# Last dense rounds of ACT and PE as engine loops, gathered rows in four paced groups, router constants loaded first

## The chip, the core and the metric

One core of a Trainium2 chip runs the whole program. The metric is the device time of one execution in microseconds. The engines are PE (TensorE), DVE (VectorE), ACT (ScalarE), POOL (GpSimd) and SP (SyncE, here a queue for transfers); they run on their own and order themselves by semaphores alone: an instruction raises a semaphore when it ends (`then_inc`), another engine waits for a value (`wait_ge`).

## What is computed

A decoder layer over x (4 batches, 512 tokens, 256 wide): a state space block, cross attention to a context, and a mixture of experts, each added to its input and normalized. The change touches the last part alone:

```python
def _ffn(x, w1, w2, w3):
    return jax.nn.silu(x @ w1.T) * (x @ w3.T) @ w2.T
shared = 0
for i in range(2):                          # two experts for all tokens
    shared = shared + _ffn(xf, sw1[i], sw2[i], sw3[i])
logits = xf @ router_w.T + expert_bias
rw, sel = jax.lax.top_k(logits, 2)          # two of eight experts for each token
rw = jax.nn.softmax(rw, axis=-1)
out = sum(combine[:, e] * _ffn(xf, w1[e], w2[e], w3[e]) for e in range(8)) + shared
x = _layernorm(x + out)
```

## The kernel before

`experts` (from L1286) works in three stages, each engine with its program in one block.

The first shared expert runs in dense rounds n = 0 to 3, one for each batch b of 512 tokens. A round has MT = 4 blocks of 128 hidden columns. PE's `hidden(n, m)` (L1805) multiplies the turned tokens by w1 and w3 into one of two PSUM buffers; each product is made of three terms of high and low parts (`xth`, `xtl`, `wh`, `wl`), so a block has 12 matmuls of 512 columns. ACT takes the silu (`activate`, L1523), DVE multiplies (`gate_on`, L1651), ACT copies the high part (`gate_high`, L1531), DVE forms the low part (`gate_low`, L1657), and PE's `down(n, m)` (L1826) multiplies by w2: 12 matmuls of 256 columns. PE's order in a round is hidden 0, 1, 2, down 0, hidden 3, down 1, 2, 3. Hidden block u waits for the gate of block u - 2. After a round DVE adds the four tiles of the result to the rows (`add_dense`, L1665), each as soon as `o_done` says so.

Beside these rounds DVE ranks the router's logits and lists the tokens of each expert. The second stage runs the chosen experts over SLOTS = 39 tiles of 128 gathered tokens: POOL gathers the rows (L1486, at most 3 tiles ahead), PE turns and multiplies them with weights addressed through a register, and SP stores each result tile to `y_dram` (L1443).

The third stage is the second shared expert: rounds n = 4 to 7, in the same form. When all result tiles are stored, POOL gathers the rows back (L1496): for each batch b, 4 tiles of tokens times 2 choices, 8 gathers of 128 rows of 1 KB, which all raise `y_fetched[b]`. The 32 gathers follow one another with no wait between. Behind them on POOL stand the four `pow` of the last normalization (L1501), one for each batch. DVE adds the gathered rows, weighted, in `add_chosen(b)` (L1683), which waits for `y_fetched[b]`, and normalizes in `normalize(b)` (L1700), which waits for POOL's `pow`. DVE's order puts these between the gates: batch 0 is added after round 5, batch 1 at (6, 2) with `normalize(0)` behind it, batch 2 at (7, 1) with `normalize(1)`, batch 3 at (7, 3) with `normalize(2)`; batch 3 is normalized last. SP stores each batch (L1446).

Ahead of the first stage SP issues, in this order, three weight loads of 512 KB (L1425), the router's weights and the bias (L1426, L1427), four stores of the rows (L1429), and the loads of all experts' weights into `wall` (L1435, "the wall loads"). PE's first transpose (L1895) waits for router and bias (`consts_loaded`); ACT splits the first weight (L1507) and then copies the turned tokens (`xth`, L1513).

Of the kernel before, what the change touches and what calls it, by code (L numbers as in the profile page):

```python
# [19 lines left out]
ACT = mybir.ActivationFunctionType  # L20
AX_X = mybir.AxisListType.X

P = 128
B, S, DM = 4, 512, 256
TT = S // P
KD = DM // P
# [1250 lines left out]
E, NSH, TOPK, HID = 8, 2, 2, 512  # L1277
MT = HID // P
NTILE = B * TT
SLOTS = B * S * TOPK // P + E - 1  # L1280
# [5 lines left out]
def experts(nc, router_t, expert_bias, w1_t, w3_t, w2_t, x2, out):  # L1286
    x2_dram = nc.dram_tensor("e_x2_dram", (NTILE * P, DM), F32, kind="Internal").ap()
    y_dram = nc.dram_tensor("e_y_dram", (SLOTS * P, DM), F32, kind="Internal").ap()
    with ExitStack() as ctx:
# [6 lines left out]
        ps_h = ctx.enter_context(nc.psum_tensor("e_h", [P, 2, 2, 512], F32))  # L1296
        ps_o = ctx.enter_context(nc.psum_tensor("e_o", [P, TT, 512], F32))

        wall = sb("e_wall", [P, E, 3, 1024])
        xth = sb("e_xth", [P, KD, B * S], F32R)  # L1300
# [112 lines left out]
        def use(n, m):  # L1413

            return n * MT + m + (SLOTS if n >= B else 0)
# [3 lines left out]
        @block.sync  # L1419
        def _(sp):  # L1420
            by_rows = lambda w, e: w[e].rearrange("(k p) n -> p k n", p=P)
            cols = (HID, HID, DM)
            tables = (w1_t, w3_t, w2_t)
            for j in range(3):
                sp.dma_start(raw_first[j].rearrange("p (k n) -> p k n", n=cols[j]), by_rows(tables[j], E)).then_inc(first_loaded[j], 16)  # L1425
            sp.dma_start(router[:], router_t.rearrange("(k p) e -> p k e", p=P)).then_inc(consts_loaded, 16)  # L1426
            sp.dma_start(bias[:], expert_bias.partition_broadcast(P)).then_inc(consts_loaded, 16)  # L1427
            for b in range(B):
                sp.dma_start(x2_dram[b * S:(b + 1) * S].rearrange("(t p) d -> p t d", p=P),  # L1429
                             x2[:, b * TT:(b + 1) * TT]).then_inc(x2_stored, 16)  # L1430
            for e in range(E):
                if e == 6:
                    sp.wait_ge(ids_done, 1)
                for j in range(3):
                    sp.dma_start(wall[:, e, j].rearrange("p (k n) -> p k n", n=cols[j]),  # L1435
                                 by_rows(tables[j], e)).then_inc(wall_loaded, 16)
            for j in range(SLOTS):
                if j in (0, 10, 18):
                    i = (0, 10, 18).index(j)
                    sp.wait_ge(w_split, 3 + i)  # L1440
                    sp.dma_start(raw[:].rearrange("p (k n) -> p k n", n=cols[i]), by_rows(tables[i], E + 1)).then_inc(raw_loaded, 16)
                sp.wait_ge(y_read, j + 1)
                sp.dma_start(y_dram[j * P:(j + 1) * P], y_row[:, j % 2]).then_inc(y_stored[j % 2], 16)  # L1443
            for b in range(B):
                sp.wait_ge(x3_ready, b + 1)
                sp.dma_start(out[b].rearrange("(t p) d -> p t d", p=P), x3[:, b * TT:(b + 1) * TT]).then_inc(stored, 16)  # L1446
            sp.wait_ge(stored, 16 * B)

        @block.gpsimd
        def _(pool):  # L1450
            nc.gpsimd.memset(ident[:], 0.0)
            nc.gpsimd.memset(lower, 1.0)
            nc.gpsimd.memset(ones, 1.0)
            nc.gpsimd.memset(before, 1.0)
            nc.gpsimd.memset(keep, 1.0)
            nc.gpsimd.memset(half[:], -0.5).then_inc(consts_set, 1)
            pool.wait_ge(consts_set, 1)
            nc.gpsimd.affine_select(out=ident[:], in_=ident[:], compare_op=ALU.not_equal, fill=1.0, base=0,
                                    pattern=[[-1, P]], channel_multiplier=1)
            nc.gpsimd.affine_select(out=lower, in_=lower, compare_op=ALU.is_gt, fill=0.0, base=0,  # L1460
                                    pattern=[[1, E], [-1, E]], channel_multiplier=0).then_inc(consts_set, 1)
            for j in range(3):
                pool.wait_ge(w_high, j + 1)
                nc.gpsimd.tensor_tensor(wl[j][:], raw_first[j], wh[j][:].bitcast(F32), ALU.subtract).then_inc(w_split, 1)
            nc.gpsimd.affine_select(out=before, in_=before, compare_op=ALU.is_gt, fill=0.0, base=0,
                                    pattern=[[1, P]], channel_multiplier=-1)
            nc.gpsimd.affine_select(out=by_expert(keep), in_=by_expert(keep), compare_op=ALU.is_gt, fill=0.0, base=0,
                                    pattern=[[0, E], [1, NTILE]], channel_multiplier=0)
            nc.gpsimd.iota(token[:], [[P, NTILE]], base=0, channel_multiplier=1, allow_small_or_imprecise_dtypes=True)
            nc.gpsimd.iota(iota[:], [[1, P]], base=0, channel_multiplier=0,  # L1470
                           allow_small_or_imprecise_dtypes=True).then_inc(consts_set, 1)

            def split_next(j):
                pool.wait_ge(raw_loaded, 16 * (j + 1))
                if j == 0:
                    pool.wait_ge(o_done, B * TT)
                nc.gpsimd.tensor_copy(wh[j][:], raw[:]).then_inc(w_high, 1)
                pool.wait_ge(w_high, 3 + j + 1)
                nc.gpsimd.tensor_tensor(wl[j][:], raw[:], wh[j][:].bitcast(F32), ALU.subtract).then_inc(w_split, 1)

            pool.wait_ge(index_ready, 1)
            pool.wait_ge(x2_stored, 16 * B)
            for j in range(SLOTS):
                if j >= XR:
                    pool.wait_ge(x_turned, j - XR + 1)
                nc.gpsimd.indirect_dma_start(x_row[:, j % XR], None, x2_dram,  # L1486
                                             bass.IndirectOffsetOnAxis(index[:, j:j + 1], 0)).then_inc(x_fetched[j % XR], 16)
                if j in (8, 16, 24):
                    split_next((8, 16, 24).index(j))
            for r in range(2):  # L1490
                pool.wait_ge(y_stored[r], 16 * ((SLOTS + 1 - r) // 2))
            for b in range(B):
                for t in range(b * TT, (b + 1) * TT):
                    for r in range(TOPK):
                        i = r * NTILE + t
                        nc.gpsimd.indirect_dma_start(y_back[:, r, t], None, y_dram,  # L1496
                                                     bass.IndirectOffsetOnAxis(place_u[:, i:i + 1], 0)).then_inc(y_fetched[b], 16)
            for b in range(B):
                rows = slice(b * TT, (b + 1) * TT)
                pool.wait_ge(var_ready, b + 1)  # L1500
                nc.gpsimd.tensor_tensor(rstd[:, rows], mv[:, rows, 1], half[:], ALU.pow).then_inc(rstd_ready, 1)  # L1501

        @block.scalar
        def _(act):
# [14 lines left out]
            def activate(u):  # L1519
                act.wait_ge(h_done, u + 1)  # L1520
                if u >= 2:
                    act.wait_ge(gate_done, u - 1)
                nc.scalar.activation(silu[:, u % 2], ps_h[:, u % 2, 0], ACT.Silu).then_inc(silu_done, 1)  # L1523

            def gate_high(n, m):
                act.wait_ge(gate_done, use(n, m) + 1)
                if n > 0:
                    act.wait_ge(o_done, n * TT)
                if n == B:
                    act.wait_ge(y_done, SLOTS)  # L1530
                nc.scalar.activation(gh[:, m], gate[:, use(n, m) % 2], ACT.Copy).then_inc(g_high, 1)  # L1531

            def read_g(j):
                act.wait_ge(g_turned, j + 1)
                if j >= 2:
                    act.wait_ge(y_done, j - 1)
                else:
                    act.wait_ge(o_done, B * TT)
                nc.scalar.activation(g_col[:, j % 2], ps_g(j), ACT.Copy).then_inc(g_read, 1)
# [7 lines left out]
            for j in range(SLOTS):  # L1547
                activate(U0 + j)
                if j >= 1:
                    read_g(j - 1)  # L1550
            for n in range(B, 2 * B):
                for m in range(MT + 1):
                    if m < MT:
                        activate(use(n, m))
                    if n == B and m == 0:
                        read_g(SLOTS - 1)
                    if m > 0:
                        gate_high(n, m - 1)

        @block.vector  # L1560
        def _(dve):
# [219 lines left out]
        def _(pe):  # L1781
# [153 lines left out]
            hidden(B, 3)  # L1935
            for m in range(1, MT):
                down(B, m)
            for n in range(B + 1, 2 * B):
                hidden(n, 0)
                hidden(n, 1)  # L1940
                hidden(n, 2)
                down(n, 0)
                hidden(n, 3)
                for m in range(1, MT):
                    down(n, m)


# [52 lines left out]
```

## Time and profile before

| | us |
|---|---|
| median of 3 runs | 3380.14 (3371.8 to 3387.71) |
| profiled execution | 3382.36 |
| its span | 3380.6 |
| PE busy | 3017.8 (89%) |
| DVE busy | 1940.5 (57%) |
| ACT busy | 1351.0 (40%) |
| POOL busy | 964.5 (29%) |

The span runs from the first to the last recorded instruction; all times in rows are from its start. The expert part begins near 2906, the chosen experts run from about 3029 to 3260, and the second shared expert from about 3252 to the end. "Idle before" and the bracket behind a row tell how long the engine had been idle and what ended that; "remote" or "another core or an unknown queue" means that the profile shows a semaphore raised but not by which instruction.

### The profile page before, as it was taken

Reading aid. Unit: us, or ns where it says so; the run is one execution under the profiler, and the core shown is the slowest. Engines: PE = TensorE matmul, PEld = TensorE weight load, DVE = VectorE, ACT = ScalarE, POOL = GpSimd, SP = SyncE. Lnnn points to the kernel's source line nnn. Section 1 sums busy time; section 2 is a strip of 40 time slices with the busy share of each in tenths; the row PEclk is TensorE's granted clock in tenths of the full one; section 3 lists DMA queues with packets and bytes.
Section 4 is the critical chain, followed back from the end, with each engine's and each line's share of the span. In section 5 each row is a group of like instructions: output and inputs, shape, how many; then the busy total and the mean of one; then the engine's idle time right before and its main releaser. Section 6 shows DMA issues by size and latency. Waiting matters only on the chain. (4 is left out here: it accounts for less than half of the span.)

```text
span 3380.6 us, 34291 instructions
## 1 busy us (share of the span) xinstructions
PE 3017.8 (89%) x11694; PEld 1872.9 (55%) x11694; DVE 1940.5 (57%) x3342; ACT 1351.0 (40%) x2320; POOL 964.5 (29%) x760
## 2 busy tenths in 40 slices
PE   6746289999999999999899999989999999799976
PEld 2212155665656565656566565656566665576655
DVE  4699466666555766665576666555555454442225
ACT  4532134445344445443544544344433434211111
POOL 1044336566101656540046666000000000102131
PEclk8878589999999999999999999999999999799997
DMA  3200344344112434231123433110111100411121
GB/s 114 89 0 0 130 127 129 103 126 132 39 35 63 129 100 134 95 104 34 51 86 125 126 104 115 33 35 14 35 22 33 42 13 13 156 55 54 50 59 37
DMA packets 90914, 248.57 MB, mean 74 GB/s; under 512 B 10660, under 2 KB 44584, under 8 KB 83064
## 3 DMA queue, kind: packets, MB, share of 16 engines
q1 hardware_dynamic: 86760, 237.04, 22.8%
q0 software_dynamic: 3408, 9.31, 1.0%
q8 instruction: 97, 1.59, 0.2%
q14 instruction: 73, 0.60, 0.1%
q10 hardware_dynamic: 576, 0.04, 0.0%
HBM read 183.34 MB, written 28.38 MB: 63 GB/s over the span
## 5 line engine op out<-in xcount | busy, mean ns | idle before, releaser
L904 ACT ACTIVATE a_p<-a_st 128x512 f32<-128x512 f32 (+1 forms) x1088 | 649.2, 597 | 1214.2 <-PE a_st L1247 1205.3
L1259 PE MATMUL a_o<-a_p,a_vals 128*65 128x512 f32 (+1 forms) x2176 | 1118.4, 596 | 0.0
L1042 DVE TENSOR_REDUCE a_maxes<-a_mx 128x1 f32<-128x512 f32 x1024 | 673.3, 682 | 112.3 <-PE a_mx L1188 106.0
L1246 PE MATMUL a_st<-a_qd,a_kodd 128*128 128x512 f32 (+1 forms) x544 | 434.7, 799 | 0.0
L1246 PE MATMUL a_st<-a_qd,a_keven 128*128 128x512 f32 (+1 forms) x544 | 434.6, 799 | 0.0
L1247 PE MATMUL a_st<-a_qm,a_kone 65*128 65x512 f32 (+1 forms) x1088 | 431.8, 397 | 0.0
L802 POOL TENSOR_TENSOR a_shared<-a_shared,a_bc 128x512 f32<-128x512 f32 x192 | 245.5, 1279 | 477.7 <-DVE a_shared L992 477.7
L1259 PEld LDWEIGHTS a_o<-a_p,a_vals 128*65 128x65 f32 (+1 forms) x2176 | 288.6, 137 | 124.5 <-issue 2.7
L1247 PEld LDWEIGHTS a_st<-a_qm,a_kone 65*128 65x128 f32 (+1 forms) x1088 | 204.1, 188 | 265.5 <-issue 265.4
L992 DVE TENSOR_TENSOR_SCAN a_shared<-a_shared 128x512 f32<-128x512 f32 x192 | 234.3, 1220 | 178.8 <-POOL a_shared L795 129.6
L795 POOL TENSOR_TENSOR a_shared<-a_dtu,a_bc 128x512 f32<-128x512 f32 x192 | 245.1, 1276 | 197.7 <-DMA a_bc<-m_kept_bc 197.7
L784 POOL TENSOR_TENSOR a_erstd<-a_emv,a_half 128x4 f32<-128x4 f32 x7 | 7.1, 1014 | 919.8 <-DVE a_emv L1068 919.6
L1144 PE MATMUL a_ring<-a_kvh,a_wt 128*128 128x512 f32 (+1 forms) x768 | 228.6, 380 | 26.7 <-POOL a_wt L820 20.7
L806 POOL TENSOR_TENSOR a_y<-a_y,a_shared 128x512 f32<-128x512 f32 x192 | 245.0, 1276 | 15.3
L1188 PE MATMUL a_mx<-a_keven,a_qd 128*128 128x512 f32 x512 | 215.3, 471 | 32.9 <-DVE a_maxes L1042 28.6
L1188 PE MATMUL a_mx<-a_kodd,a_qd 128*128 128x512 f32 x512 | 218.8, 452 | 28.9 <-DVE a_maxes L1042 28.3
L1035 DVE COPY a_vals<-a_ring 128x512 f32<-128x512 f32 (+2 forms) x160 | 97.6, 610 | 235.8 <-PE a_ring L1144 234.9
L1246 PEld LDWEIGHTS a_st<-a_qd,a_kodd 128*128 128x128 f32 (+1 forms) x544 | 101.7, 187 | 160.2 <-issue 118.7
L1246 PEld LDWEIGHTS a_st<-a_qd,a_keven 128*128 128x128 f32 (+1 forms) x544 | 101.7, 187 | 159.2 <-issue 103.9
L1144 PEld LDWEIGHTS a_ring<-a_kvh,a_wt 128*128 128x128 f32 x768 | 142.3, 192 | 67.1 <-issue 21.1
L1523 ACT ACTIVATE e_silu<-e_h 128x512 f32<-128x512 f32 x71 | 42.4, 597 | 334.5 <-PE e_h L1865 185.5
L1651 DVE TENSOR_TENSOR e_gate<-e_silu,e_h 128x512 f32<-128x512 f32 x71 | 48.7, 686 | 220.5 <-ACT e_silu L1523 217.3
(242 smaller groups left out, 4451.6 us busy)
## 6 DMA issues: line engine op xcount, KB each, us to landing
a_bc<-m_kept_bc SPq DMA_DIRECT2D x192, 512.0 KB, 3.7
a_wt<-a_w_split SPq DMA_DIRECT2D x15, 1536.0 KB, 9.4
a_kone<-a_keven SPq DMA_DIRECT2D x32, 528.5 KB, 5.0
a_kone<-a_kodd SPq DMA_DIRECT2D x32, 528.5 KB, 5.5
e_wall<-in_w_t_dram SPq DMA_DIRECT2D x27, 512.0 KB, 5.2
a_shared<-in_ctx_dram SPq DMA_DIRECT2D x4, 1536.0 KB
a_w_split<-a_wt SPq DMA_DIRECT2D x4, 1536.0 KB, 6.5
a_dtu<-m_kept_dtu SPq DMA_DIRECT2D x12, 512.0 KB, 4.9
```

What stands on the lines that cost most here:

```text
L795: nc.gpsimd.tensor_tensor(dbx[:, n % 2], dtu[:, c % 2, 1], bc[:, n % 2, 0], ALU.mult).then_inc(dbx_ready, 1)
L802: nc.gpsimd.tensor_tensor(seen, state[:, n % 2], bc[:, n % 2, 1], ALU.mult).then_inc(seen_ready, 1)
L806: nc.gpsimd.tensor_tensor(y[:, c], y[:, c], seen, ALU.add).then_inc(y_added, 1)
L904: nc.scalar.activation(p[0:r, s % 4], st[0:r, s % 2], ACT.Exp, scale=SCALE).then_inc(exp_done, 1)
L992: nc.vector.tensor_tensor_scan(state[:, n % 2], decay[:, n % 2], dbx[:, n % 2], 0.0, ALU.mult, ALU.add).then_inc(scanned, 1)
L1035: o = nc.vector.tensor_copy(vals[0:r, t * HG:(t + w) * HG, 0:DH], made)
L1042: nc.vector.reduce_max(maxes[:, c, t:t + 1], mx[:, i % 2], AX_X).then_inc(mx_max, 1)
L1144: mm = nc.tensor.matmul(out, x(k), y(k), start=(j == 0), stop=(j == len(terms) - 1))
L1188: mm = nc.tensor.matmul(mx[:, i % 2], qd[of(g)][:, t * P:(t + 1) * P], kk[:, c * 512:(c + 1) * 512], start=True, stop=True)
L1246: nc.tensor.matmul(st[0:r, s % 2], keys_of(g)[:, kt * P:kt * P + r], qd[of(g)][:], start=True, stop=False)
L1247: nc.tensor.matmul(st[0:r, s % 2], k_one[g % 2][0:DH + 1, kt * P:kt * P + r], qm[of(g)][0:DH + 1, :], start=False, stop=True).then_inc(st_ ...
L1259: nc.tensor.matmul(ps_o[0:DH + 1, g % 2], vals[0:r, kt * HG + j, :], p[0:r, s % 4], start=(kt == 0), stop=(kt == KT - 1)).then_inc(pv_done, 1)
```

## The change

Three things. In PE's and ACT's programs the rounds n = 5, 6 and 7, written out instruction by instruction before, become a loop of the engine over n; wait values and the column range of the tokens are computed in registers from n. ACT's round n = 4 and PE's stay written out. On POOL the gathers of batch b > 0 wait until all of batch b - 1 have landed. On SP the two small loads of the router stand before the three weight loads. What is computed is the same.

```diff
-            for j in range(3):
-                sp.dma_start(raw_first[j]..., by_rows(tables[j], E)).then_inc(first_loaded[j], 16)
             sp.dma_start(router[:], router_t.rearrange("(k p) e -> p k e", p=P)).then_inc(consts_loaded, 16)
             sp.dma_start(bias[:], expert_bias.partition_broadcast(P)).then_inc(consts_loaded, 16)
+            for j in range(3):
+                sp.dma_start(raw_first[j]..., by_rows(tables[j], E)).then_inc(first_loaded[j], 16)
...
             for b in range(B):
+                if b > 0:
+                    pool.wait_ge(y_fetched[b - 1], 16 * TT * TOPK)
                 for t in range(b * TT, (b + 1) * TT):
                     for r in range(TOPK):
...
-            for n in range(B, 2 * B):
+            for m in range(MT + 1):
+                if m < MT:
+                    activate(use(B, m))
+                if m == 0:
+                    read_g(SLOTS - 1)
+                if m > 0:
+                    gate_high(B, m - 1)
+            with act.Fori(B + 1, 2 * B) as n:
                 for m in range(MT + 1):
+                    u = n * MT + m + SLOTS
                     if m < MT:
-                        activate(use(n, m))
...
+                        act.wait_ge(h_done, u + 1)
+                        act.wait_ge(gate_done, u - 1)
+                        nc.scalar.activation(silu[:, (SLOTS + m) % 2], ps_h[:, (SLOTS + m) % 2, 0], ACT.Silu).then_inc(silu_done, 1)
                     if m > 0:
-                        gate_high(n, m - 1)
+                        act.wait_ge(gate_done, u)
+                        act.wait_ge(o_done, n * TT)
+                        nc.scalar.activation(gh[:, m - 1], gate[:, (SLOTS + m - 1) % 2], ACT.Copy).then_inc(g_high, 1)
...
-            for n in range(B + 1, 2 * B):
-                hidden(n, 0)
...
+            with pe.Fori(B + 1, 2 * B) as n:
+                def hidden_last(m):
+                    u = n * MT + m + SLOTS
+                    pe.wait_ge(gate_done, u - 1)
+                    for part, (h, l) in enumerate(((w1h, w1l), (w3h, w3l))):
+                        terms = [(x, y, k) for x, y in ((h, xth), (h, xtl), (l, xth)) for k in range(KD)]
+                        for i, (x, y, k) in enumerate(terms):
+                            mm = nc.tensor.matmul(ps_h[:, (SLOTS + m) % 2, part], x[:, k, m * P:(m + 1) * P],
+                                                  y[:, k, bass.ds((n - B) * S, S)], start=(i == 0), stop=(i == len(terms) - 1))
+                    mm.then_inc(h_done, 1)
+
+                def down_last(m):
+                    pe.wait_ge(g_low, n * MT + m + 1)
+                    for t in range(TT):
+                        if m == 0:
+                            pe.wait_ge(o_read, (n - 1) * TT + t + 1)
+                        for i, (x, y) in enumerate(((gh, w2h), (gh, w2l), (gl, w2h))):
+                            mm = nc.tensor.matmul(ps_o[:, t, 0:DM], x[:, m, t * P:(t + 1) * P], y[:, m],
+                                                  start=(m == 0 and i == 0), stop=(m == MT - 1 and i == 2))
+                        if m == MT - 1:
+                            mm.then_inc(o_done, 1)
+
+                hidden_last(0)
...
+                    down_last(m)
```

## Rows read from the trace of the kernel before

**Rows 1.** The page's slices: PE's granted clock in tenths, 40 equal slices.
```profile
PEclk8878589999999999999999999999999999799997
```
**Rows 2.** Windows: stretch, length, busy us of each engine, clock, DMA share, GB/s.
```profile
3100.00:3200.00 100.00, 100.00 (x381) 62.12 (x381) 24.84 (x52) 18.48 (x35) 22.91 (x21) 1.00 0.17 51
...
3270.00:3309.00 39.00, 8.60 (x48) 7.30 (x48) 2.91 (x7) 1.17 (x2) 25.64 (x27) 0.65 0.33 94
...
3331.00:3353.00 22.00, 19.26 (x100) 17.00 (x101) 13.60 (x34) 4.59 (x9) 1.85 (x2) 0.92 0.07 25
```
**Rows 3.** The chain that ended last, from 3260: start us, us, what.
```profile
3269.97 38.30 another core or an unknown queue
```
**Rows 4.** Waits, 3265 to 3309: who waited for whom, total us, times, longest.
```profile
ACT e_silu L1523 <- remote: 37.7, 1, 37.7
```
**Rows 5.** Timeline of PE around 3273 to 3315: start us, us, instruction.
```profile
3273.54 0.63 PE L1805 MATMUL e_h<-e_xth,e_wh 128*128 128x512 f32 x2
...
3276.28 0.62 PE L1805 MATMUL e_h<-e_xth,e_wh 128*128 128x512 f32 x2
...
3278.78 0.39 PE L1805 MATMUL e_h<-e_xth,e_wl 128*128 128x512 f32 x1
3309.73 1.22 PE L1805 MATMUL e_h<-e_xth,e_wh 128*128 128x512 f32 x2 [30.57 <-DVE e_gate L1651]
...
3315.02 0.41 PE L1826 MATMUL e_o<-e_wh,e_gh 128*128 128x256 f32 x1
```
**Rows 6.** Timeline of DVE, the additions of round 4, first and last of four.
```profile
3277.43 0.42 DVE L1665 TENSOR_TENSOR rows<-e_o,rows 128x256 f32<-128x256 f32 x1 [6.13 <-remote]
...
3285.20 0.42 DVE L1665 TENSOR_TENSOR rows<-e_o,rows 128x256 f32<-128x256 f32 x1 [3.11 <-remote]
```
**Rows 7.** Timeline of ACT, its first silu after the stall.
```profile
3308.29 0.60 ACT L1523 ACTIVATE e_silu<-e_h 128x512 f32<-128x512 f32 x1 [37.72 <-remote]
```
**Rows 8.** Timeline of POOL, first and last of the 32 gathers.
```profile
3264.00 0.95 POOL L1496 DMA_INDIRECT e_wall<-e_y_dram,e_place_u  x1 [39.28 <-DMA e_y_dram<-e_y_row]
...
3302.86 0.95 POOL L1496 DMA_INDIRECT e_wall<-e_y_dram,e_place_u  x1 [0.30 <-issue]
```
**Rows 9.** Timeline, 3016 to 3018: third gather of x rows, ACT's silu beside it.
```profile
3016.50 1.10 POOL L1486 DMA_INDIRECT e_x_row<-e_x_dram,e_index  x1 [0.30 <-issue]
...
3017.51 0.60 ACT L1523 ACTIVATE e_silu<-e_h 128x512 f32<-128x512 f32 x1 [1.60 <-PE e_h L1805]
```
**Rows 10.** DMA: queues in 3262 to 3266, in 3270 to 3309; x gathers to landing.
```profile
q8 instruction: 1, 0.02, 2.2%
q14 instruction: 1, 0.01, 0.7%
...
q0 software_dynamic: 1347, 3.67, 32.7%
...
e_x_row<-e_x_dram,e_index POOLq DMA_INDIRECT x5, 3.7
```
**Rows 11.** Timeline of DVE: the gathered rows of batch 1 added, (6, 2).
```profile
3336.32 3.37 DVE L1683 SCALAR_TENSOR_TENSOR rows<-e_wall,e_weight,rows 128x256 f32<-128x256 f32 x8
```
**Rows 12.** Waits, 3310 to the end.
```profile
PE e_h L1805 <- DVE e_gate L1651: 31.6, 2, 30.6
...
PE e_o L1826 <- DVE e_gl L1657: 8.1, 4, 3.0
...
DVE e_wall L1700 <- POOL e_rstd L1501: 1.1, 1, 1.1
```
**Rows 13.** Timeline of SP, PE and ACT where the expert part starts.
```profile
2908.82 0.77 SPq L1427 DMA_DIRECT2D e_bias<-in_expert_bias_dram  x1
...
2914.31 1.94 PE L1895 MATMUL e_h<-e_ident,rows 128*128 128x128 f32 x8 [13.35 <-DMA e_bias<-in_expert_bias_dram]
...
2911.06 1.06 ACT L1507 ACTIVATE e_wh<-e_wall 128x1024 fp32r<-128x1024 f32 x1 [12.94 <-DMA e_wall<-in_w_t_dram]
2915.44 0.60 ACT L1513 ACTIVATE e_xth<-e_h 128x512 fp32r<-128x512 f32 x1 [3.32 <-PE e_h L1895]
```

More of the change, by code:

```diff
@@ L1423, in _ @@
             tables = (w1_t, w3_t, w2_t)
+            sp.dma_start(router[:], router_t.rearrange("(k p) e -> p k e", p=P)).then_inc(consts_loaded, 16)
+            sp.dma_start(bias[:], expert_bias.partition_broadcast(P)).then_inc(consts_loaded, 16)
             for j in range(3):
                 sp.dma_start(raw_first[j].rearrange("p (k n) -> p k n", n=cols[j]), by_rows(tables[j], E)).then_inc(first_loaded[j], 16)
-            sp.dma_start(router[:], router_t.rearrange("(k p) e -> p k e", p=P)).then_inc(consts_loaded, 16)
-            sp.dma_start(bias[:], expert_bias.partition_broadcast(P)).then_inc(consts_loaded, 16)
             for b in range(B):
@@ L1550, in _ @@
                     read_g(j - 1)
-            for n in range(B, 2 * B):
+            for m in range(MT + 1):
[6 more added lines that the diff above has]
+            with act.Fori(B + 1, 2 * B) as n:
                 for m in range(MT + 1):
+                    u = n * MT + m + SLOTS
                     if m < MT:
-                        activate(use(n, m))
-                    if n == B and m == 0:
-                        read_g(SLOTS - 1)
+                        act.wait_ge(h_done, u + 1)
+                        act.wait_ge(gate_done, u - 1)
+                        nc.scalar.activation(silu[:, (SLOTS + m) % 2], ps_h[:, (SLOTS + m) % 2, 0], ACT.Silu).then_inc(silu_done, 1)
                     if m > 0:
-                        gate_high(n, m - 1)
+                        act.wait_ge(gate_done, u)
+                        act.wait_ge(o_done, n * TT)
+                        nc.scalar.activation(gh[:, m - 1], gate[:, (SLOTS + m - 1) % 2], ACT.Copy).then_inc(g_high, 1)
         @block.vector
@@ L1937, in _ @@
                 down(B, m)
-            for n in range(B + 1, 2 * B):
-                hidden(n, 0)
[L1940 to L1943, printed above, removed]
+            with pe.Fori(B + 1, 2 * B) as n:
[19 more added lines that the diff above has]
+                hidden_last(0)
+                hidden_last(1)
+                hidden_last(2)
+                down_last(0)
+                hidden_last(3)
                 for m in range(1, MT):
-                    down(n, m)
+                    down_last(m)
 def laid_out(x, ctx_1024, L0_attn_W_in, L0_attn_conv_w, L0_attn_conv_b, L0_attn_W_x, L0_attn_W_dt, L0_attn_b_dt,
```

## The prediction

> **What bounds the kernel now.** I read the page's forty slices first, in them the granted clock of PE, which is full nearly throughout and falls twice in the last six slices [rows 1]; the clock falls where PE stands, and the changed rounds lie there. The windows by stage place it: in 3100 to 3200 PE is busy for 100.00 of 100 us, in 3270 to 3309 for 8.60 of 39 us at a mean granted clock of 0.65, and in 3331 to 3353, one dense round, for 19.26 of 22 us [rows 2]. The chain that ended last has one piece of 38.30 us at 3269.97 which it puts down to "another core or an unknown queue" [rows 3]. The waits of 3265 to 3309 name a releaser of the same kind, "remote", for ACT: 37.7 us in one wait [rows 4].
>
> The timeline shows what that is. PE runs the first hidden block of round n=5 from 3273.54 and the second from 3276.28, and ends at 3278.78 + 0.39 = 3279.17; it starts again at 3309.73, and says it waited 30.57 us for DVE's gate [rows 5]. DVE waited for ACT's silu, and ACT for PE's own `h_done` of the first block, whose last matmul had begun before 3276.28. DVE's additions of round n=4 (L1665), which need only PE's `o_done` from before 3273.54, start at 3277.43 and, for the last of four, 3285.20, both after a wait on "remote" [rows 5, 6]. ACT resumes at 3308.29 [rows 7]. So PE's work was done and its signals took 4 to 32 us to be acted on. Beside it POOL issues 32 row gathers (L1496), the first at 3264.00, the last at 3302.86, so 1.25 us apart [rows 8]; ACT goes on 5.4 us after the last issue. The three gathers at the start of the chosen experts end without such a delay: the third is issued at 3016.50 and ACT's silu starts at 3017.51 after an ordinary 1.60 us wait on PE [rows 9]. My reading: PE's signals are held while a long unbroken burst of gathers runs. The first one seen late is that of the first addition, due near 3272.6 (the last down block of 1.4 us ends at 3273.54), when seven gathers had been issued.
>
> **The change part by part.** *Pacing (L1492 to 1496).* POOL now waits for each group of 8 gathers to land before it issues the next. It removes nothing. A group takes 7 x 1.25 = 8.75 us from first to last issue, then the landing: 3.7 us from issue in the gathers of x rows [rows 10], hence a period of some 12.5 us. Last issue: 3 x 12.5 + 8.75 = 46.3 us after the first, against 38.9 now, 7.4 us later. If a burst of 8 lets go of PE's signals when it drains, PE goes on at 3279.17, since the gate of (5,0) would be there (3276.45 + 0.60 + 0.69 = about 3278). That is 30.6 us. PE also restarts warm: the first block after the stall takes 3315.02 - 3309.73 = 5.29 us, the warm one 3276.28 - 3273.54 = 2.74 us [rows 5], 2.5 us more. Together **-33.1 us**.
>
> What is late next. Queued behind POOL's new waits are the four `pow` (L1501), and DVE's `normalize(0)` waits for the first of them. Now DVE reaches the preceding addition of round (6,2) at 3336.32 [rows 11] and normalizes 3.4 us later, at 3339.7. With -33.1 and the start's -1.8 that is 3304.8, but POOL is free only at 3262.2 + 46.3 + 1.0 = 3309.5, plus 1.0 for the `pow`: DVE waits up to 5.7 us there with the gate of (6,3) behind it, and PE with that. The other thing left is signals held in the last few us of each burst, perhaps 2 us of PE for each of three groups, up to 4. These two cover each other in part: **+6 us**, bounds 4 and 12. The rows themselves arrive in time: group 3 lands near 3312, and DVE wants it in round (7,3), a round of 22 us [rows 2] after (6,3), so not before 3325.
>
> *Loops on ACT and PE.* The same matmuls and activations run. Added are register arithmetic for wait values and for four addresses of the moving operand, and two back edges on each engine. The trace has no such wait. From below: in the chosen experts PE addresses the weights by register and still is busy 100.00 of 100 us [rows 2], so hidden work costs 0. From above: 0.30 us, the part of the 1.25 us between two unwaited gathers in which POOL is not busy (0.95 busy) [rows 8], on each of the 28 register waits of a round (12 on PE, 16 on ACT), times three: 25 us. Only waits that end last count. After 3310 PE waits 4 times for `gl` and once more for the gate besides the stall [rows 12], and each passes through ACT as well: about 10 x 0.3 = **+3 us**, bounds 0 and 25. The cover is PE's queue running ahead during the 2.74 us hidden blocks.
>
> Is code loading what stalls ACT? The last instruction transfers before the stall, one of each queue, lie in 3262 to 3266, and in 3270 to 3309 the only queue with packets is the gathers' [rows 10]. No engine asks for code there, so shorter code cures nothing by itself. The Trainium skill (Runtime: NRT & Kernel Launch, Instruction fetch mechanics) says an engine fetches its next block while it runs the present one; by that rule a late block would bite at a block's end, and the trace, with a fetch just made, speaks against a code stall. The same section speaks against the loops: a taken branch whose target has left the two-page window forces a fetch. No run here shows that; by it the loops would cost up to four more transfers, which the fourth case below bounds from rows.
>
> *Router constants first.* PE's first transpose (L1895) starts at 2914.31, when the bias lands, 5.5 us after an issue at 2908.82 behind three weight loads; ACT converts weight 0 at 2911.06 and then idles until its first `xth` at 2915.44 [rows 13]. Ahead of the weights the two small loads should land near 2910. They push every later load of SP (three weights, four stores of x2, 18 wall loads) back by some 1.3 us (each load takes SP 0.5 to 0.8 us to issue), so ACT's conversion ends at 2911.06 + 1.3 + 1.06 = 2913.4 and `xth` starts there, 2.0 us earlier; ACT's order then keeps 1.8. The wall loads are waited for only at the chosen experts, long after. **-1.8 us**, bounds -3 (the whole idle) and +1.3 (only the weights' delay is felt).
>
> **Sum.** -33.1 - 1.8 + 6 + 3 = -25.9 us on the span of 3380.6: 3354.7, and 1.8 us more as execution time (3382.4 now): 3356.5. The profiled run lies 2.2 us above the median of 3380.1, so the median should be near 3354. About 0.5% (17 us, 3363) is what a measurement of this kernel can tell from no change.
>
> **The rivals.**
> A. *The forecast, pacing frees PE.* With the bounds, 3344 to 3368. For: three gathers in a row cost nothing. Against: a burst of 8 is one longer than what preceded the first late signal. Chance 0.56, of which 0.52 lies below 3363.
> B. *Signals are held through each burst and let go only in the gaps.* Then each gap moves PE by about one block and the waiting signals; by the last group round n=5 is done. PE restarts 7.4 - 1.8 = 5.6 us later than now, with one round of 22 us [rows 2] behind it: -22 + 5.6 + 3 = -13.4, so 3367. For: the four `o_done` come singly, 2.6 us apart on average [rows 6]. Chance 0.12, within 0.5%.
> C. *The hold lasts until all gathers are over.* The gaps (under 4 us) are too short to clear it; the release came 5.4 us after the last issue. Then nothing of the stall goes: +5.6 + 3 = +8.6, so 3389. The same time would follow if the change rested on a code-load stall that isn't there. Chance 0.20, within 0.5%.
> D. *The other side: slower.* C, and the loop's back edges load code again while the gathers run: four back edges at a transfer's 3.7 us [rows 10] are 15 us, or the register waits reach half of their upper bound. From 11 us of loop cost beyond C's 3 it decides: 3380 + 8.6 + 11 = 3400, up to 3407. Chance 0.12.
>
> **How the numbers follow.** Likeliest 3354. Faster 0.52, within 0.5% 0.04 + 0.12 + 0.20 = 0.36, slower 0.12. The range 3344 to 3391 takes in A, B and C and leaves out D and the far edges, about 0.15.
>
> **What would show each step.** Pacing: in the profile after, L1496 in four bursts with three idles of about 3 us released by DMA; the 38 us piece gone from the chain; PE's granted clock 1.00 through 3270 to 3309. B: four short stalls of PE spaced 12.5 us. C: one stall to about 3314. The new POOL wait: DVE's L1700 waiting some us for `e_rstd` (1.1 us in all now [rows 12]). Loops: the dense rounds n=6 and 7 longer than 22 us beyond the `e_rstd` wait, or an idle at L1805 at a round's head. Constants: PE's L1895 waiting about 9 us, not 13.35 [rows 13], and ACT's first `xth` near 2913.4. The forecast is wrong if the hold is neither tied to the length of the burst nor cleared by a gap of some 3 us.

## The result and the profile after

The changed kernel takes 3353.31 us, the median of six runs (3349.9 to 3358.08), where the kernel before takes 3381.97 (six runs, 3371.8 to 3387.71): a ratio of 0.991, with a 95% interval of 0.9896 to 0.9925. The forecast was 3354. The profiled execution took 3351.15 us, its span is 3349.4, 31.2 us less than before's 3380.6.

Its granted clock in the forty slices. Where [rows 1] fell to 7 in the sixth slice from the end, it now reads 8; the rest is nearly the same:
```profile
PEclk8878589999999999999999999999999999899998
```
The windows, with the columns of [rows 2]: a stretch that the stall does not touch, then the 39 us in which the stall lay (taken 4 us earlier, since POOL's first gather comes 3.9 us earlier), then the 22 us behind it.
```profile
3100.00:3200.00 100.00, 100.00 (x380) 61.78 (x380) 24.55 (x51) 18.62 (x35) 20.30 (x20) 1.00 0.17 52
3266.00:3305.00 39.00, 34.13 (x181) 29.35 (x181) 20.13 (x47) 8.13 (x14) 25.67 (x27) 0.96 0.31 88
3305.00:3327.00 22.00, 18.67 (x98) 16.11 (x96) 14.62 (x39) 4.58 (x8) 3.01 (x3) 0.92 0.11 36
```
PE, busy for 8.60 of these 39 us before, is busy for 34.13, at a mean granted clock of 0.96 in place of 0.65. POOL and the transfers do as much as before (25.67 against 25.64 us, 88 against 94 GB/s): what stopped PE was not the amount of the transfers.

POOL's timeline around the waits: the first gather, the last of group 0, the first of groups 1, 2 and 3, the last of all, and the `pow` behind it.
```profile
3260.14 0.94 POOL L1498 DMA_INDIRECT e_wall<-e_y_dram,e_place_u  x1 [39.29 <-DMA e_y_dram<-e_y_row]
...
3269.01 0.94 POOL L1498 DMA_INDIRECT e_wall<-e_y_dram,e_place_u  x1 [0.30 <-issue]
3272.04 0.94 POOL L1498 DMA_INDIRECT e_wall<-e_y_dram,e_place_u  x1 [2.09 <-DMA e_wall<-e_y_dram,e_place_u]
...
3284.19 0.94 POOL L1498 DMA_INDIRECT e_wall<-e_y_dram,e_place_u  x1 [2.06 <-DMA e_wall<-e_y_dram,e_place_u]
...
3296.31 0.94 POOL L1498 DMA_INDIRECT e_wall<-e_y_dram,e_place_u  x1 [2.10 <-DMA e_wall<-e_y_dram,e_place_u]
...
3305.23 0.95 POOL L1498 DMA_INDIRECT e_wall<-e_y_dram,e_place_u  x1 [0.30 <-issue]
3306.20 1.05 POOL L1503 TENSOR_TENSOR e_rstd<-e_mv,e_half 128x4 f32<-128x4 f32 x1
```
Four bursts with three idles of 2.1 us, released by the transfers, 12.1 us apart. The chain that ended last, from 3265 on, has no piece of an unknown releaser where [rows 3] had one of 38.30 us. It runs along POOL's gathers and their landings into the first `pow` and DVE's `normalize(0)` (L1712, L1700 before), and from there through the gate to PE (start, us, what):
```profile
3269.01 2.77 DMA e_wall<-e_y_dram,e_place_u
...
3281.18 2.75 DMA e_wall<-e_y_dram,e_place_u
...
3293.27 2.78 DMA e_wall<-e_y_dram,e_place_u
...
3306.20 1.06 POOL e_rstd L1503
3307.36 1.02 DVE e_wall L1712 x3
3308.65 0.68 DVE e_gate L1663
3309.33 0.61 DVE e_gl L1669
3309.99 4.35 PE e_o L1967 x24
```
So the new bound of this stretch is the wait that the change adds, as the forecast's "what is late next" had it. The signals are not wholly free either. The waits of 3250 to 3350 (who waited for whom, total us, times, longest), against 37.7 us in one wait in [rows 4]:
```profile
ACT e_silu L1566 <- PE e_h L1957: 41.4, 10, 9.4
...
POOL e_wall L1498 <- DMA e_wall<-e_y_dram,e_place_u: 6.2, 3, 2.1
ACT e_silu L1566 <- remote: 6.0, 2, 5.7
DVE rows L1677 <- remote: 4.2, 1, 4.2
...
DVE e_wall L1712 <- POOL e_rstd L1503: 2.3, 2, 1.2
```
Three waits on "remote" are left, two of ACT and one of DVE. The timelines of DVE, ACT and PE show where signals come late, first the addition of round n=4, then silus, then the end of PE's block (6,0):
```profile
3271.65 1.42 DVE L1677 TENSOR_TENSOR rows<-e_o,rows 128x256 f32<-128x256 f32 x4 [4.22 <-remote]
```
```profile
3278.06 0.60 ACT L1566 ACTIVATE e_silu<-e_h 128x512 f32<-128x512 f32 x1 [1.52 <-PE e_h L1957]
...
3295.00 0.60 ACT L1566 ACTIVATE e_silu<-e_h 128x512 f32<-128x512 f32 x1 [9.38 <-PE e_h L1957]
3295.85 0.60 ACT L1566 ACTIVATE e_silu<-e_h 128x512 f32<-128x512 f32 x1 [0.25 <-remote]
...
3307.72 0.60 ACT L1566 ACTIVATE e_silu<-e_h 128x512 f32<-128x512 f32 x1 [5.75 <-remote]
```
```profile
3290.89 0.61 PE L1957 MATMUL e_h<-e_xth,e_wl 128*128 x2
3291.34 0.62 PE L1957 MATMUL e_h<-e_xth,e_wh 128*128 x2
...
3296.44 0.73 PE L1957 MATMUL e_h<-e_xth,e_wh 128*128 x2 [2.22 <-DVE e_gate L1663]
```
Block (6,0) ends when PE's next one begins, near 3291.5, and its silu starts at 3295.00, 3.5 us behind that and 1.7 us after the last issue of group 2 (3293.27); the silu of block (6,1), which ends at 3294.2, starts at 3295.85. All late places (these two, the additions from 3271.65, the silus at 3283.58 and 3307.72) have a signal due between the sixth gather of a burst and 1 us behind its last, and start 1.7 to 2.6 us behind the last issue. The silu at 3278.06, five gathers into group 1, is on time. So each burst of eight still delays signals, but for 1 to 4 us, and they are through by the time the group lands, 2.8 us after its last issue.

What exactly is late? The trace also has the time at which each semaphore was raised. In the kernel before, PE's block (5,0) ends at 3276.45 and its `h_done` is raised at 3308.27; the four `o_done` of round 4, due from 3272.62 to 3273.70, are raised at 3277.40, 3279.54, 3281.64 and 3285.18, while POOL goes on issuing. ACT and DVE start within 0.03 us of these times. So it is PE's semaphore that rises late, and not the waiting engine that answers late. DVE's own signal of its second addition, due at 3279.99 in the same stretch, is raised at 3280.00. And the word "held" says too much for `o_done`: during the burst these signals pass, one by one. The last gather packet ends at 3305.27, so the stall ends 3.0 us behind the transfers, where after a burst of eight no signal came later than the landing.

At the start, PE's first transpose and ACT's first `xth`, to be laid beside [rows 13]:
```profile
2905.22 0.39 SPq L1424 DMA_DIRECT2D e_router<-in_router_t_dram  x1
...
2908.61 3.62 PE L1907 MATMUL e_h<-e_ident,rows 128*128 128x128 f32 x16 [9.25 <-DMA e_bias<-in_expert_bias_dram]
2910.31 1.06 ACT L1509 ACTIVATE e_wh<-e_wall 128x1024 fp32r<-128x1024 f32 x1 [14.18 <-DMA e_wall<-in_w_t_dram]
2911.28 0.58 ACT L1515 ACTIVATE e_xth<-e_h 128x512 fp32r<-128x512 f32 x1
```
PE waits 9.25 us and not 13.35. The stages ahead of the change had already run 1.6 us shorter in this execution, which is not the change's.

Where the 31.2 us of span went: 1.6 ahead of the expert part; 2.3 between it and POOL's first gather (counted from SP's first load of the part, 2906.81 before and 2905.22 after: from 3264.00 - 2906.81 = 357.19 to 3260.14 - 2905.22 = 354.92); and 27.3 from the first gather to the end (3380.6 - 3264.00 = 116.60 before, 3349.4 - 3260.14 = 89.26 after). That last length, "first gather to end", is the yardstick of the experiments, since only the last part of the program is in it.

### The profile page after: what moved, and what is told of

Read it like the earlier page. It is cut to its first block and busy times, and to the rows that moved or that the text cites. A ratio compares the mean times of both kernels' runs of the same rounds, so it can differ in the third digit from the quotient of the medians.

```text
span 3349.4 us, 34358 instructions
## 1 busy us (share of the span) xinstructions
PE 3011.7 (90%) x11690; PEld 1869.2 (56%) x11694; DVE 1942.5 (58%) x3342; ACT 1350.9 (40%) x2320; POOL 965.4 (29%) x760
## 5 line engine op out<-in xcount | busy, mean ns | idle before, releaser
L1144 PE MATMUL a_ring<-a_wt,a_kvh 128*128 128x256 f32 (+1 forms) x1088 | 174.1, 282 | 0.0
L1144 PEld LDWEIGHTS a_ring<-a_wt,a_kvh 128*128 128x128 f32 (+1 forms) x1088 | 158.5, 187 | 14.5
```

Of the source, the lines that this page charges most:

```text
L1144: mm = nc.tensor.matmul(out, x(k), y(k), start=(j == 0), stop=(j == len(terms) - 1))
```

## The experiments

The forecast rests on one theory, S: PE's signals are held while a long burst of gathers runs, and a gap lets them go. The first rival, L: the engines lose the time to loading code, and the loops cure it. Each comparison is with runs of the kernel before on the same chip.

**One part at a time.** Four kernels: pacing alone, loops alone, constants alone, pacing and constants. `pace_only` is the kernel before with

```diff
             for b in range(B):
+                if b > 0:
+                    pool.wait_ge(y_fetched[b - 1], 16 * TT * TOPK)
```

> The kernel before with the pacing alone. Theory S (PE's signals are held while a long burst of gathers runs, and a drained group of 8 lets them go): the stall of 38 us in the chain goes and the time falls by 24 to 29 us, to about 3355, some 3 us of it from not having the loops. Theory L (the stall comes from loading the written-out code of ACT and PE, and only the loops cure it): the stall stays and moves with the end of the gathers, 3382 to 3390 us. Theory B (both are needed): between, 3365 to 3380.

`loops_only` has the two `Fori` loops and neither of the other parts.

> The kernel before with the two loops alone, gathers unpaced. Theory S: the stall stays whole (PE idle about 30 us from 3279, ended near 3308), time 3382 to 3388 us, the loops costing 0 to 5 us. Theory L: the stall goes, 3350 to 3356 us, and the four o_done of round 4 are answered within 1 us.

`pace_consts` is the changed kernel with the rounds n = 5 to 7 written out as before.

> The changed kernel with its two loops written out again (pacing and router constants first stay). If the loops cost what the forecast took (3 us), this is 3 us faster than the changed kernel: about 3350 us; if they cost nothing, 3353; if they are what helps, over 3360.

`consts_only` moves the two small loads:

```diff
+            sp.dma_start(router[:], ...).then_inc(consts_loaded, 16)
+            sp.dma_start(bias[:], ...).then_inc(consts_loaded, 16)
             for j in range(3):
                 sp.dma_start(raw_first[j]..., by_rows(tables[j], E)).then_inc(first_loaded[j], 16)
-            sp.dma_start(router[:], ...).then_inc(consts_loaded, 16)
-            sp.dma_start(bias[:], ...).then_inc(consts_loaded, 16)
```

> The kernel before with the router's two loads first, nothing else. The forecast: 1.8 us less, about 3380 us, too little to tell in the median but to be seen in the trace: ACT's first xth 1.8 to 2.6 us earlier after SP's first load, the first gather of the result rows as much earlier. Rival: the weight loads are 1.3 us later and ACT gains nothing; then the distance from SP's first load to the first gather is as before (357.2 us).

Measured, with the kernel before at 3349.11 us on this chip, not 3382:

| kernel | us | ratio (95%) | first gather to end |
|---|---|---|---|
| pace_only | 3356.33 | 1.0022 (1.0009 to 1.0034) | 88.46 |
| loops_only | 3348.67 | 0.9991 (0.9979 to 1.0002) | 82.04 |
| pace_consts | 3352.26 | 1.0017 (1.0004 to 1.003) | 88.41 |
| consts_only | 3348.53 | 0.9993 (0.9983 to 1.0003) | 83.56 |

Neither theory had this. On this chip the stall isn't there at all, with the long burst in place in two of the four kernels. In `consts_only`, whose last part is that of the kernel before, the window around the gathers and three of ACT's silus in it:
```profile
3266.00:3305.00 39.00, 36.20 (x207) 31.31 (x205) 22.63 (x52) 10.39 (x18) 29.11 (x30) 1.00 0.36 102
```
```profile
3280.07 0.60 ACT L1523 ACTIVATE e_silu<-e_h 128x512 f32<-128x512 f32 x1 [1.60 <-PE e_h L1805]
3284.25 0.60 ACT L1523 ACTIVATE e_silu<-e_h 128x512 f32<-128x512 f32 x1 [3.06 <-PE e_h L1805]
3292.21 0.60 ACT L1523 ACTIVATE e_silu<-e_h 128x512 f32<-128x512 f32 x1 [5.91 <-PE e_h L1805]
```
PE is busy for 36.20 of 39 us at full clock, the transfers run at 102 GB/s, faster than in [rows 2], and no wait names "remote". So the four kernels could not tell S from L, but each gives the bare price of its part. Pacing costs 5.6 us where there is nothing to cure (the mean of 88.46 and 88.41, less that of 82.04 and 83.56), or 4.9 us between `pace_consts` and `consts_only`, which differ in pacing alone. Of the 1.5 us by which `loops_only` is below `consts_only`, 1.3 lie in a drop of the granted clock: it is 0.62 in `consts_only` from 3306 to 3309, in the last blocks of round 6, and 1.00 at that place in `loops_only`. The price is one wait, in `pace_consts`:
```profile
3299.61 2.98 DVE L1685 SCALAR_TENSOR_TENSOR rows<-e_wall,e_weight,rows 128x256 f32<-128x256 f32 x7
3307.54 1.38 DVE L1702 TENSOR_SCALAR e_wall<-rows,e_mv,e_rstd 128x256 f32<-128x256 f32 x4 [4.96 <-POOL e_rstd L1503]
3308.84 0.68 DVE L1653 TENSOR_TENSOR e_gate<-e_silu,e_h 128x512 f32<-128x512 f32 x1
```
DVE stands 4.96 us at `normalize(0)` until POOL, through with its paced gathers, has done the `pow`; the gate of (6,3) stands behind it.

**The two theories where the stall is.** On another chip the kernel before took 3385.6 us. There the changed kernel was run again, beside one without pacing:

```diff
# loops_consts, against the changed kernel
             for b in range(B):
-                if b > 0:
-                    pool.wait_ge(y_fetched[b - 1], 16 * TT * TOPK)
```

> The changed kernel once more, beside the kernel before. In the last four runs the kernel before took 3349 us, not 3382, and no stall was in any profile. Theory C (the hold of PE's signals belongs to the chip): where the kernel before takes about 3349 us, the changed one takes 3350 to 3355, within 0.3% of it, and its profile shows PE's signals answered at once; where before takes about 3380, it takes 3350 to 3358. Theory P (the hold belongs to the build of the kernel before, and comes back with it on any chip in some loads): before is near 3380 again and the changed kernel near 3350.

> The changed kernel without the pacing (loops and router constants first stay). Where before takes 3349 us: 3344 to 3349, and some 5 us under the changed kernel, because DVE no longer waits for the first pow behind the paced gathers (4.96 us with pacing). Where before takes 3380 us: theory S (a long burst holds PE's signals) expects the whole stall, 3375 to 3385; theory L (code loading) expects 3345 to 3352.

`changed_again` took 3358.78 us, 0.9919 (0.9903 to 0.9936), with 89.04 us from first gather to end. `loops_consts` took 3381.86 us, 0.9989 (0.9979 to 0.9999), with 117.34 us. Its chain, its waits and ACT's timeline:
```profile
3272.72 38.94 another core or an unknown queue
```
```profile
ACT e_silu L1564 <- remote: 38.5, 1, 38.5
...
DVE rows L1675 <- remote: 18.2, 4, 8.3
...
PE e_h L1955 <- DVE e_gate L1661: 30.9, 2, 29.9
```
```profile
3311.77 1.09 ACT L1564 ACTIVATE e_silu<-e_h 128x512 f32<-128x512 f32 x2 [38.54 <-remote]
```
With both loops in place the whole stall stays (38.94 us beside [rows 3]'s 38.30, PE idle for 29.9 beside 30.57 in [rows 5]). L falls: shorter code cures nothing. With the loops in place, pacing takes 117.34 - 89.04 = 28.3 us out, all of the gain. P falls as well as far as it meant the build of the kernel before: `loops_consts` is another build and has the stall. One case is not closed: pacing without the loops met no chip with the stall, so that the rival of `pace_only`'s expectation by which both are needed is not excluded. No trace speaks for it. S stands, with a condition that it didn't have: the hold is there in the comparisons on some chips and not in those on others.

The signals of `loops_consts` come as in the kernel before: its four `o_done`, due from 3275.28 to 3276.36, are raised at 3282.23, 3285.03, 3288.53 and 3293.45, further and further apart, and the `h_done` due at 3279.11 is raised at 3311.66, 32.6 us late and 3.8 us behind the last gather packet. PE itself runs slower just before it stops, at a full granted clock: it is idle 0.47 and 0.31 us within block (5,1) with no wait in the profile. In the ten profiles of the comparisons without a stall (those below included), no `h_done` or `o_done` due from 3262 to 3330 is more than 0.02 us late, by the same records.

**Can the pace's own price go?** `early_pow` is the changed kernel with the first `pow` ahead of the last group on POOL:

```diff
             for b in range(B):
                 if b > 0:
                     pool.wait_ge(y_fetched[b - 1], 16 * TT * TOPK)
+                if b == 3:
+                    pow_of(0)          # waits for var_ready >= 1, then the pow of batch 0
                 for t in range(b * TT, (b + 1) * TT):
...
-            for b in range(B):
+            for b in range(1, B):
```

> The changed kernel with the pow of batch 0 issued on POOL ahead of the last group of gathers. The forecast's step (DVE's normalize(0) waits for the pow behind the gathers, up to 5.7 us): where no signals are held (the kernel before near 3349 us), DVE's 5 us wait for e_rstd goes and the time falls by 4 to 5 us against the changed kernel, to about 3347 to 3350; where they are held (before near 3383), the wait was only 1.2 to 2.9 us and 1 to 3 us go. Rival: POOL then waits for var_ready(0) and holds the last group back, no gain.

The chip had no stall (before: 3347.76). `early_pow` took 3347.11 us, 1.0002 (0.9992 to 1.0012), with 3343.1 - 3261.34 = 81.76 us from first gather to end. Its DVE no longer waits at that place:
```profile
3300.06 3.38 DVE L1700 SCALAR_TENSOR_TENSOR rows<-e_wall,e_weight,rows 128x256 f32<-128x256 f32 x8
3303.47 1.38 DVE L1717 TENSOR_SCALAR e_wall<-rows,e_mv,e_rstd 128x256 f32<-128x256 f32 x4
```
The price of the pacing goes with this wait, and the gaps between the groups are free, by the last part; the rival (POOL held back by the early `pow`, no gain) is out. The changed kernel itself did not run beside it.

`fours_early_pow` has gaps after every four gathers and the early `pow`:

```diff
+                        done = t * TOPK + r
+                        if done and done % 4 == 0:
+                            pool.wait_ge(y_fetched[(done - 1) // (TT * TOPK)], 16 * ((done - 1) % (TT * TOPK) + 1))
```

> The same with eight groups of 4 gathers. The longest unbroken burst is then 5 us. Where signals are held: if the hold needs more than four gathers in a row, no signal of PE is late and the time is 3 to 6 us below the changed kernel, if not for POOL being busy some 8 us longer; if each burst holds from its second gather on, lateness stays. Where none are held: within 3 us of early_pow.

3348.14 us, 1.0005 (0.9994 to 1.0017), 82.47 us from first gather to end; the last issue is 52.9 us after the first. On a third chip without a stall (before: 3350.21) the same kernel:

> Eight groups of 4 gathers with the early pow, once more, in the hope of a chip on which the kernel before takes about 3383 us. There: if the hold needs more than four gathers in a row, no signal of PE is over 1 us late and the time is 3350 us or less, 4 us or more under the changed kernel beside before (0.991); if each burst holds, about the changed kernel's ratio. Where the kernel before takes 3348 us it says nothing new: ratio 1.000.

3347.72 us, 1.0002 (0.9991 to 1.0014), 83.69 us. The 1.2 us between the two are again a drop of the granted clock in the last blocks of round 6: 0.54 from 3304 to 3307 in `fours_again`, 1.00 at that place in `fours_early_pow`. Smaller groups cost nothing, while whether four at a time removes the held 1 to 4 us could not be seen here.

`window_2` keeps at most two gathers under way: each waits for the one two before it.

> As early_pow, but with no groups: each gather waits for the one two before it, so two are under way at any time and there is no pause. Theory D (the hold builds up with gathers queued, and goes when they drain): little or no lateness, as only two are queued. Theory G (any traffic of gathers without a gap of 2 us holds the signals): the stall is back, 20 us or more, on a chip where the kernel before has it.

One execution: 3346.22 us, beside 3347.76 for before, and 3344.5 - 3262.72 = 81.8 us from first gather to end. No cost is seen either; between D and G it says nothing, since the chip had no stall.

**Is it POOL's queue?** `sp_plain` takes POOL's 32 gathers away and lets SP issue 32 plain transfers of the same size, the rows of result tile i in place of those that the tokens' places name:

```diff
-                        nc.gpsimd.indirect_dma_start(y_back[:, r, t], None, y_dram, ...place_u[:, i:i + 1]...)
+                        sp.dma_start(y_back[:, r, t], y_dram[i * P:(i + 1) * P])   # on SP, ahead of its stores
```

> The kernel before with the 32 row gathers of POOL replaced by 32 plain transfers of the same size from SP's queue, which fetch the rows of tile i in order and not the chosen ones. Theory Q (it is POOL's queue, with descriptors made by software, that holds PE's signals): no signal late, and some 30 us less than the kernel before on a chip where that takes 3383. Theory T (it is the traffic into the same tile): the stall stays.

> Plain transfers of the same size from SP's queue in place of POOL's gathers, once more (they fetch the rows of tile i in order, not the chosen ones). On a chip where the kernel before takes 3383 us: theory Q (POOL's queue with descriptors made by software holds PE's signals) expects about 3350 and no wait on remote; theory T (the traffic does) expects 3375 to 3385. Where before takes 3348 us: no difference.

`sp_plain` took 3346.41 us in one execution (before: 3347.76); `sp_plain_again`, on the third chip without a stall, took 3348.02, 1.0001 (0.9988 to 1.0014). From SP's first of these transfers to the end it is 82.5 and 80.8 us. Both are as fast as the burst of gathers where that holds nothing. SP issues its 32 transfers in 16.1 and 16.3 us, 0.5 us apart, where POOL takes 1.25 us for each, so the two bursts differ in pace as well as in queue. These two runs were meant for a chip with the stall and met none, so whether a long burst of another queue holds signals as well stays open.

## Why the prediction came out

**The stall: the mechanism held, and its price.** The forecast took off 30.6 us of idle PE and 2.5 us of cold restart, 33.1 in all. Last parts with the hold take 116.60 and 117.34 us, those without it and without pacing 82.04 and 83.56: 34.2 us between the means. Reading [rows 5 to 8] as held signals, and not as a slow engine or as code, was right: the stall goes with the unbroken burst, by `loops_consts` and `changed_again`, and the records of the semaphores show the late signals themselves. The reading of [rows 10] against code loading was right too: shortening the code left the 38.94 us where they were. No run contradicts the rule that the prediction cited from the Trainium skill (Runtime: NRT & Kernel Launch, Instruction fetch mechanics), that the next block of code is fetched while the present one runs.

**The step that was missing: where the hold comes.** Nothing in the trace of before told that the hold is not always there. The prediction treated it as this kernel's property. It came out because both kernels were timed where the hold is, and that was luck. Where it is not, the changed kernel itself was not run, but `pace_consts`, which is all of it but the loops, is slower, at 1.0017 (1.0004 to 1.003). There the first term of the forecast is nothing, and what is left is a loss.

**Leftovers, +6.** The changed kernel takes 89.26 and 89.04 us from first gather to end, 6.4 more than the mean of 82.8 without hold or pacing. The step named both parts and said that they cover each other, and they do: where nothing is held DVE waits 4.96 us for the `pow` (forecast: up to 5.7); where signals are held at the bursts' ends, DVE comes later to that point and waits 1.2 us in the profile of after and 2.9 in `changed_again`, with nearly the same length in all.

**Loops, +3: mis-sized, it is 0.** `loops_only`'s last part is the shortest of the first four (82.04, 1.3 us of that by the clock), and `early_pow`, also with loops, has 81.76. Block by block the silus of `loops_only` and `consts_only` keep the same distances to 0.1 us up to (6,3). The term failed at its first assumption: the 0.30 us between POOL's gathers isn't what a register wait costs PE or ACT while their queue is ahead. The lower bound, PE at 100.00 of 100 us with addresses by register in [rows 2], was the nearer row. The taken branches, against which the same section of the Trainium skill warns, cost nothing that any run here shows.

**Constants, -1.8.** Counted from the start of the expert part, ACT's first `xth` comes at 2911.28 - 2905.22 = 6.06 us, where it was 8.63 (2915.44 - 2906.81): -2.6, more than forecast (2.0 for the `xth`, of which 1.8 was kept): the weight was pushed back by 0.8 us (2910.31 - 2905.22 = 5.09, from 2911.06 - 2906.81 = 4.25) and not by 1.3. Up to the first gather the changed kernel is 2.3 us shorter, but other kernels without the move are as short as it: the length up to the last result store differs by up to 4 us between executions: from SP's first load to the first gather it is 353.1 us in `pace_only`, without the move, and 357.2 in before, and over the first four twelfths of that way the granted clock is 0.56, 0.96, 1.00 and 0.88 in the one and 0.50, 0.94, 1.00 and 0.83 in the other. `consts_only` as a whole, 0.9993 (0.9983 to 1.0003), is not told from no change. The 2.6 us are shown at the start of the part, not at the end of the program.

**The pacing's own times.** A group lands 2.8 us after its last issue, where 3.7 were taken from the gathers of x rows, so the period is 12.1 us (forecast 12.5) and the last issue is 45.1 us after the first (46.3). The `pow` comes 1.2 us earlier than forecast, and the wait where nothing is held is 4.96 and not 5.7.

**Sum.** With -34.2, +6.4, 0 and -2.3 (the way to the first gather, whatever shortened it) the sum is -30.1, and with the 1.6 us of the earlier stages -31.7, beside 31.2 measured. The forecast of -25.9 in the span was 3.7 us short of the part that the change can move (29.6): 3 us of it are the loops. For the profiled execution the forecast was 3356.5, and it took 3351.15: 5.3 too much (these 3.7 and the 1.6). The median came out within 1 us of the forecast all the same, since after's profiled run lies 2.2 us below its median where before's lay 2.2 above the one then known; that is 4.4 us of luck. One figure of the prediction doesn't follow from its own terms: with their bounds added up, rival A runs from 3348 to 3385, and not from 3344 to 3368.

Of the rivals, B (held to the gaps) asked for four stalls of PE, and C for one up to 3314; PE's 34.13 busy us of 39 exclude both. D fell with the loops' cost.

**What stays open.** Why signals are held in some comparisons and not in others (each was on one chip at one time, so that the chip and its condition of the moment are not told apart); whether pacing would do without the loops where the hold is; whether the signal alone is late or the last write of PE's result before it, since the ends of PE's matmuls are modelled in the trace; whether the recording of the trace has a part in it, since each execution here was recorded and has a span and a clock of its own, and records are lost where signals are late (see the end); whether the count of gathers or the time of the burst sets the first late one (seven before, six or more here); whether groups of four or a plain queue would be free of it; and what `early_pow` takes where the hold is. If its 5 us of wait are gone there but the held 1 to 4 us are not, some of the 6.4 us should return; that was not measured. Of the kernels run, `early_pow` is the one to keep, as far as is known: it has the changed kernel's gaps, and where nothing is held its last part is 81.8 us in place of 88.4.

## What to carry to other kernels

When an engine has ended its work in the timeline and the next one waits for a "remote" release, look at what a third engine issues in an unbroken row at that time: a gap every eight issues gave back 28 us of 34 here, and where nothing was held it cost nothing once the work queued behind the paced issues had been moved ahead of the last group. Run the kernel before anew with each comparison, since such a stall need not be there everywhere, and then price the cure also where there is nothing to cure. Take for a new kind of instruction the row nearest in engine and state: a loop on PE was priced rightly by PE's own addressed matmuls and wrongly by POOL's gaps. Lay the time at which a semaphore was raised against the end of the instruction that raises it: that tells a late signal from a late answer.

## What the hardware showed

- PE's signals were held during 32 gathers in a row in two comparisons (the kernel before at 3382 and 3386 us). In a third, on another chip than the second, two kernels with the same unbroken row have no late signal (before at 3349 us); in two more, on two other chips, the kernel before took 3348 and 3350 us, so that by its time it had no stall there either. Within a comparison the kernel before kept to its level: no execution of 19 in the two lies under 3371 us, none of 71 in the three over 3359. The hold is worth 34 us.
- Where signals are held in a long row, PE's semaphores rise 4.8 to 32.6 us after its matmuls end: `o_done` one by one while the row goes on, `h_done` only 3.0 to 3.8 us behind the last gather packet. DVE's own signals in the same stretch rise on time (due at 3279.99, raised at 3280.00 in before; due at 3282.68, 3285.47 and 3288.98, raised within 0.02 us in `loops_consts`).
- A burst of eight, 8.9 to 9.2 us from first to last issue, delays signals by 1 to 4 us at its end; signals due while five or fewer had been issued came in time.
- In these runs some records of raised semaphores are missing: in the last part, from 3262 to 3345, 6 to 12 of 70 to 101 of seven semaphores of PE, ACT and DVE, in each of the four profiles with late signals, against 0 to 2 of 100 to 108 in the four kernels that were run one part at a time. None of the held ones is among them. "Remote" and "another core or an unknown queue" stand in the profile of this program of one core because the record comes so long after the end of the matmul that raised it.
- Three rounds as a loop on PE of 96 matmuls and as many weight loads, with two back edges and waits against registers, took the same time as when written out, to 0.1 us in a block.
